# An attention kernel with hyperbolic distances: pairs of key tiles added by accumulating DMAs, the feed-forward products moved later, and another order at the end

## The reference

```python
xn = layernorm(x)
q, k, v = xn @ Wq.T, xn @ Wk.T, xn @ Wv.T          # 16 heads of 32
diff_sq = max(|q|^2 + |k|^2 - 2 q.k, 0)
denom = max((1 - |q|^2) * (1 - |k|^2), 1e-6)
distance = arccosh(1 + 2 * diff_sq / denom)
attn = softmax(-distance, axis=-1)
out = x + (attn @ v) @ Wo.T + xn @ quantise_int4(kernel) + bias + (xn @ a) @ b
```

## Time and profile before

| | us |
|---|---|
| median of 3 runs | 2315.15 (2313.09 to 2316.01) |
| the profiled execution's own time | 2314.24 |
| its span in the trace | 2312.4 |
| TensorE busy | 2201.1 (95%) |
| VectorE busy | 2083.9 (90%) |
| ScalarE busy | 2074.4 (90%) |
| GpSimd busy | 313.4 (14%) |
| DMA engines, mean share in the span | 43.0% for SP's queue |

### The profile page before, as it was taken

The page is one execution under the profiler, slowest core; times in us unless marked ns, Lnnn a source line. Parts: engine busy times, 40 slices in busy tenths (PEclk is TensorE's granted clock), DMA queues, the critical chain, the costliest instruction groups (busy, mean ns, idle before and its releaser), DMA issues.

```text
span 2312.4 us, 45533 instructions
## 1 busy us (share of the span) xinstructions
PE 2201.1 (95%) x17416; PEld 863.7 (37%) x17416; DVE 2083.9 (90%) x2794; ACT 2074.4 (90%) x1909; POOL 313.4 (14%) x193
## 2 busy tenths in 40 slices
PE   6999999999999999999999999999999999988886
PEld 2443333334343434434334433343433444322222
DVE  7779898999999999999999999999999999888987
ACT  4379999999999999999999999999999999999992
POOL 0101111111111111111111111111111111100003
PEclk9999999999999999999999999999999999999998
DMA  4354332534545343455425354453344543344433
GB/s 145 118 146 114 100 108 68 154 112 134 145 137 140 104 131 109 142 140 143 133 86 151 105 151 131 125 158 101 116 126 146 136 141 110 87 119 103 123 96 96
DMA packets 355428, 285.04 MB, mean 123 GB/s; under 512 B 81132, under 2 KB 294252, under 8 KB 355208
## 3 DMA queue, kind: packets, MB, share of 16 engines
q1 hardware_dynamic: 355208, 282.10, 43.0%
HBM read 159.77 MB, written 121.36 MB: 122 GB/s over the span
## 4 chain that ended last, share of the span: by engine, by line
PE 56%; ACT 19%; issue 11%; DVE 10%; SPq 2%; DMA 2%; POOL 1%; ACTq 0%; DVEq 0%; POOLq 0%
PE pM L305 20%; PE pU L225 12%; PE pO L237 11%; ACT root L529 9%; ACT root L535 8%; PE pZ L253 6%; DVE root L871 3%; DVE root L866 2%; PE pM L295 2%; ACT qk L556 1%; SPq L1112 1%; PE pM L278 1%; PE pO L305 1%; DVE kx L739 1%; PE pM L281 1%
## 5 line engine op out<-in xcount | busy, mean ns | idle before, releaser
L529 ACT ACTIVATE root<-pU 128x1024 f32<-128x1024 f32 x1008 | 1016.9, 1039 | 78.2 <-PE pU L225 72.8
L535 ACT ACTIVATE root<-root 128x2048 f32<-128x2048 f32 x512 | 989.5, 1933 | 46.0 <-DVE root L866 46.0
L866 DVE TENSOR_SCALAR root<-root 128x2048 f32<-128x2048 f32 (+1 forms) x512 | 647.0, 1264 | 71.5 <-ACT root L529 71.2
L225 PE MATMUL pU<-QS,KS 100*128 100x512 f16 x2048 | 610.6, 381 | 40.9 <-ACT root L529 37.2
L871 DVE TENSOR_TENSOR root<-root 128x2048 f32<-128x2048 f32 x256 | 586.2, 2290 | 1.0 <-PE pO L237 0.9
L237 PE MATMUL pO<-root,VX 128*32 128x512 f32 x4096 | 505.8, 607 | 7.8 <-ACT root L535 7.7
L1018 POOL TENSOR_TENSOR sqr<-qk 128x512 f32<-128x512 f32 x112 | 208.5, 1862 | 997.0 <-ACT qk L556 910.9
L225 PEld LDWEIGHTS pU<-QS,KS 100*128 100x128 f16 x2048 | 175.2, 98 | 384.0 <-issue 143.4
L253 PE MATMUL pZ<-root,ones 128*32 128x512 f32 x2048 | 269.3, 597 | 18.3 <-DVE root L871 18.3
L237 PEld LDWEIGHTS pO<-root,VX 128*32 128x32 f32 x4096 | 103.9, 109 | 283.9 <-issue 191.4
L1013 POOL TENSOR_TENSOR xts<-xts,bias_b 128x512 f32<-128x512 f32 x64 | 82.9, 1297 | 680.2 <-PE pM L295 622.9
(11 more groups left out here) (228 smaller groups left out, 2210.3 us busy)
## 6 DMA issues: line engine op xcount, KB each, us to landing
v_d<-v_o SPq DMA_DIRECT2D x64, 264.0 KB, 2.1
k_d<-kx SPq DMA_DIRECT2D x64, 264.0 KB, 2.1
KT<-k_d SPq DMA_DIRECT2D x64, 264.0 KB
VX<-v_d SPq DMA_DIRECT2D x64, 264.0 KB
xts<-in_x SPq DMA_DIRECT2D x32, 512.0 KB, 4.3
res_d<-f_o SPq DMA_DIRECT2D x64, 256.0 KB, 3.9
QS<-qh_d SPq DMA_DIRECT2D x128, 128.0 KB
KS<-kh_d SPq DMA_DIRECT2D x128, 128.0 KB
```

What stands on the lines that cost most here:

```text
L225: mm = pe.matmul(pU[:, col:col + HALF], KS[i][:, h, j * P:(j + 1) * P], QS[i][:, h, half * HALF:(half + 1) * HALF], start=True, stop=True)
L529: act.activation(root[:, q % RING, cols], pU[:, cols], ACT.Square).then_inc(squared, 1)
L535: act.activation(root[:, q % RING, :], root[:, q % RING, :], ACT.Sqrt).then_inc(rooted, 1)
L866: v.tensor_scalar(root[:, q % RING, cols], root[:, q % RING, cols], CS * CS, CS * CS, ALU.max, ALU.subtract).then_inc(clamped, 1)
```

## The change

1. In periods 8 to 55 (`HELD`) the sum of the first pair of tiles goes into a buffer of its own, `held`. The sums of the second and third pair are added to it by two DMAs that GpSimd issues, 1 MB each, with `accum_op`; the second waits for the first. TensorE sums the held tiles and the fourth pair by ones, one after the other, at the end of the period. The ring of `root` becomes one of four for even and one of three for odd tiles (`slot`), with waits of its own (`wait_free`).
2. The feed-forward products (`feed`) no longer use the transposed tile at hand. SP stores each transposed and split tile in device memory (`xT_d`) and loads it again 15 periods after its projection (`F_LAG`); `x` for the residual is loaded again too. Nothing of `f` is left in the prologue. The quantising and folding of its weights is spread in pieces over periods 0 to 6. The last eight products run in periods 56 to 63, beside those of the lagging tiles. The result of `take_f` stays in SBUF (`xr`) for the output (`take_o` reads it there); it is still stored to `res_d`, but no longer loaded from it.
3. `divide` works on one row tile in every period instead of two in every even one.
4. At the end, GpSimd issues the loads for the last block's first three groups itself, the division of tiles 56 and 57 comes after the last pair is added, and GpSimd's last division waits for it.

The order of the prologue's banks changes with this.

```diff
+        HELD = range(LEAD, LATE)
+        def slot(q):
+            return 4 + q // 2 % 3 if q % 2 else q // 2 % 4
+        def wait_free(engine, q):
+            u = q - 6 if q % 2 else q - 8
+            if u < 0:
+                return
+            p, j = u // JC, u % JC
+            if j % 2:
+                engine.wait_ge(pair_added, u // 2 + 1)
+                engine.wait_ge(v_summed, u + 1)
+            elif p not in HELD or j == 6:
+                engine.wait_ge(summed_up, u + 2)
+            elif j == 0:
+                engine.wait_ge(pair_added, u // 2 + 1)
+            else:
+                engine.wait_ge(accumulated, 16 * (2 * (p - HELD[0]) + j // 2))
...
             def sum_one(q):
                 p, j = q // JC, q % JC
+                first = j == (JC - 1 if p in HELD else 1)
+                if p in HELD and not first:
+                    return
                 pe.wait_ge(pair_added, q // 2 + 1)
...
+                if p in HELD:
+                    pe.wait_ge(accumulated, 32 * (p - HELD[0] + 1))
+                    for h in range(G4):
+                        pe.matmul(pZ[h * HD:(h + 1) * HD, :], ones[:, :], held[:, h * HALF:(h + 1) * HALF], start=True, stop=False)
...
             def add_pair(q):
...
+                if q // JC in HELD and q % JC == 1:
+                    v.wait_ge(summed_up, q // JC * JC)
+                    into = held[:, :]
+                v.tensor_tensor(into, even, root[:, slot(q), :], ALU.add).then_inc(pair_added, 1)
...
             def divide(n):
-                v.wait_ge(raw_loaded, (n // 2 + 1) * 5 * 16)
+                v.wait_ge(raw_loaded, (n + 1) * 5 * 16)
...
+            def accumulate(p, i):
+                q = p * JC + 2 * i + 1
+                g.wait_ge(pair_added, q // 2 + 1)
+                if i == 2:
+                    g.wait_ge(accumulated, 16 * (2 * (p - HELD[0]) + 1))
+                g.dma_start(held[:, :], root[:, slot(q - 1), :], accum_op=ALU.add).then_inc(accumulated, 16)
...
             for n in range(LEAD, NT):
+                if n - LEAD - 1 in HELD:
+                    accumulate(n - LEAD - 1, 2)
                 square_qk(n, 0)
                 square_qk(n, 1)
...
-                add_bias(n)
+                if n >= LEAD + F_LAG:
+                    g.wait_ge(featT_made[0], n + 1)
+                    add_bias(n - LEAD - F_LAG)
+                if n - LEAD in HELD:
+                    accumulate(n - LEAD, 1)
...
+            load_three()
             divide_three()
             divide_two()
...
+                elif k in (0, 1, 2):
+                    if k == 0:
+                        pe.wait_ge(taken["o"], o)
+                        pe.wait_ge(feat_split[1], NT)
+                    feed(p, 0, 4 * k, 4 * k + 4)
```

More of the change, by code:

```diff
@@ L312, in project, with feed, low_rank_rows @@
                     mm.then_inc(made[k], 1)
+            def feed(m, b, first, last):
+                late = m >= NT - LEAD
+                t = xT[m % 2] if late else fT[m % 2]
+                if first == 0 and late:
+                    pe.wait_ge(fT_late[m % 2], ((m - NT + LEAD) // 2 + 1) * 16)
+                elif first == 0:
+                    pe.wait_ge(fT_loaded[m % 2], (m // 2 + 1) * 16)
+                if m == 0 and first == 0:
+                    pe.wait_ge(w_low, 4)
+                mm = product(pM[b], lambda c: t[:, 0, c, :], lambda c: t[:, 1, c, :], W["f"], first, last)
+                if last == 3 * KC:
+                    mm.then_inc(made["f"], 1)
+            def low_rank_rows(c, b):
+                if c == 0:
+                    pe.wait_ge(rank_loaded, 2 * 16)
+                pe.matmul(pM[b][:, :], At[:, c * P:(c + 1) * P], Bl, start=True, stop=True).then_inc(low_rank, 1)
             def output(o, b, first, last):
-                cols = slice(o % 2 * P, (o % 2 + 1) * P)
-                mm = product(pM[b], lambda c: ah[:, c, cols], lambda c: al[:, c, cols], W["o"], first, last)
+                mm = product(pM[b], lambda c: ah[:, c, :], lambda c: al[:, c, :], W["o"], first, last)
                 if last == 3 * KC:
@@ L584, in behind @@
                 n = p + LEAD
-                if p == 2 and k == 8:
+                if p == 3 and k == 13:
+                    high(4, "f", 3)
+                if p == 5 and k == 13:
                     high(3, "o", 4)
```

595 lines of the change are left out of this document (333 added, 262 removed).

## The result

The changed kernel takes 2461.55 us (median of 4 runs, 2458.65 to 2477.46), the kernel before 2315.58 (4 runs, 2313.09 to 2316.86). The ratio is 1.065, with a 95% interval of 1.062 to 1.068. The forecast was 2237 us, its range 2195 to 2350. The profiled execution has a span of 2457.9 us.

A forecast was written before the change was run, and what follows sets the result against it. TensorE was taken as the bound in periods 8 to 55, with ScalarE and VectorE near. Sum: 2314 - 31 - 3 - 37 + 3 - 9 = 2237 us; range 2195 to 2350.

The forecast's parts named there:

- Step 1: Periods 8 to 55: two fewer sums of ones by TensorE, saving it 1.72 us a period.
- Step 2: Periods 8 to 55, division by 128-row tiles: a pair of periods takes 66.2 us against 67.8, 37 us less over 23 pairs.
- the forecast's lower bound: Periods 8 to 55: if engines lend each other time, VectorE's sum decides, 64.6 us a pair, 74 us less.
- Step 3: Two accumulating DMAs per period: landings of 6.9 and 11.3 us, 18.2 together, right at the limit; cost taken nothing.
- the stack loads can yield: Argument against late accumulates: loads of the next stack on the DMA queues can give way to them; no size given.
- Rival A: Accumulates are late, TensorE waits in 48 periods; break-even 1.6 us a period, 2381 us at 3 over the slack; chance 0.21.
- Rival B: GpSimd's lists and VectorE's in-order waits eat the gain: a period back to 33.9 us, total 2274; chance 0.16.
- Step 4: Feed-forward product leaves the prologue: 31 us less, bounds 24 to 34; periods 0 to 6 another 3 us less.
- Step 5: Periods 56 to 63 take eight returned products, 3 us more; period 63 and the last addition 9 us less, bounds 0 to 14.
- my bound of +10: Upper bound on the 3 us more for the feed-forward products returning at the end, bounds -3 to +10.

## Why the prediction was wrong, point by point

**Step 1, the saved sums: right in kind, a little large.** TensorE's work in periods 8 to 55 falls by 1608.5 - 1544.0 = 64.5 us, 1.3 a period instead of 1.7, when the transfers are tiny. **Step 2, the pair of periods: right.** 66.2 was forecast, 66.4 is measured there, 66.8 in the undisturbed pairs of the changed kernel. The engines behind it were the other way round: VectorE has 33.4 us in the even periods and 31.8 in the odd ones, where I had 30.8 and 33. Without accumulates the division begins 30.7 or 31.4 us into a period, so each one's work falls largely into the next period, and the sum of the two, 65.2, is near the 64.6 of the forecast's lower bound.

**Step 3, the accumulating DMAs: the failed step.** Its own question was answered well. I took 6.9 and 11.3 us for the two landings, 18.2 in all; they took 7.0 to 11.6, 8.5 at the median, 17 us for two, and the wait for `held` came to 23 us in 48 periods, half a us each. The step failed where it says "Cost taken: nothing" and, with SyncE's issues, "if those are held up, TensorE waits for at most the 2.5 us of five issues in the odd periods". The only price I gave a transfer was its own landing against the one instruction that waits for it. I used the full queues (share 0.98 in the earlier trace rows) to lengthen the accumulates, and never the other way: that 5.3 us of all sixteen engines, twice a period, would push back the transfers already there. The rows for it stood in the prediction: a DMA share of 0.77 and 0.78 in the odd periods, to which 10.6 of 33 us, 0.32, was to be added (0.27 by the prediction's own 4.4 us of the queues' time for each, which was mis-sized a little). Either way the sum is above 1. The two sets of small or urgent transfers that this hits, the key sums at the end of the even periods and the feature stores with the stacks behind them, cost 115 us of TensorE's waits, 125 with the late `xT`. The bound of 2.5 us failed with it: one wait for the key sums reached 6.7 us, since both their issues and their landing became slower. I wrote "the stack loads can yield"; in the first period of every eight they could not.

**A second term was missing**: after such a wait the clock is low (0.50 in the windows of 1244 to 1250 us), and the same matmuls took 48 us more.

**Rival A** had the right sign for a near cause, late accumulates by 1.6 us a period or more; its chance, 0.21, was the only weight on this side. Its mechanism was not the main one: what it describes is 23 us of waits for `held` and 42 of ScalarE's for ring slots, which TensorE feels in part. **Rival B** (VectorE held up by GpSimd's lists) came only in small: VectorE's clamps took 1.37 us on average in periods 8 to 55 against 1.28 without accumulates, 0.8 us a period, its additions 2.28 and 2.27.

**Step 4, the prologue: right.** The loop's first square starts at 110.9 us instead of 139.3, 28.4 us less for 31 forecast; periods 0 to 7 take 2.1 us less for 3.

**Step 5, the end: the sum was mis-sized.** Periods 56 to 62 took 12.9 us more (6.5 with no and 10.7 with tiny transfers) where I had 3. TensorE has 1736 matmuls there instead of 1544 and is busy 200 us instead of 169: fourteen feed-forward products, not seven, since besides the last eight those of the lagging tiles end there too (tile m's product stands in period m + 7). I had counted eight over all eight periods. With 2.6 us for each of fourteen the sum is 168.8 + 36.4 = 205 us, above the 201.9 of before, and VectorE (196) and ScalarE (195) are as near, so that little is lent; my bound of +10 would have been the value. Period 63 and the end brought 7.4 us for 9; period 63 itself took 29.6 us.

With the transfers free the changed kernel takes 2252 us, 15 us from 2237, so the other steps were near together. The bytes made the other 209.5.

## What to carry to other kernels

A DMA costs not only its own landing: add the engine time of a new transfer to the DMA share of each stretch in which it runs, and where the sum passes 1 (here 0.78 + 0.32), look for small or urgent transfers of other queues that are issued beside it and for who waits for them in order. An addition by DMA took here twice the engine time of a copy. Weigh that against what the engine work that it takes away is worth in time: here 25 us for 96 transfers, while the rest of the change, without them, made the kernel 1.8% faster.

## What the runs showed of the hardware

- A 1 MB addition by GpSimd's DMA from SBUF to SBUF held the sixteen DMA engines for 5.3 us and landed 8.5 us after its issue at the median (7.0 to 11.6); a plain copy 2.7 and 5.5 us.
- A transfer of some hundred bytes on SyncE's queue, issued 1.4 us behind such an addition's own issue, landed when the addition was through, 5.7 us later, and TensorE waited for this last one of sixteen.
- Beside two such additions a period, sixteen small issues on SyncE took 12.8 us at the median instead of 10.5 (no accumulates).
- While GpSimd added 128x2048 numbers (5.4 us), an addition of 128x2 on VectorE took 4.31 us instead of 0.16.
- Six us without matmuls were followed by 6 us at the clock's lower level, 1.2 GHz (granted clock 0.50).
